# Projections of two small-head layers placed in steps without products with values, and tiles of ones written by ScalarE

## The reference

```python
# layer 1: 16 heads of 16, 256 queries, 256 keys, a mask on keys; then an MLP (gelu, 256 -> 1024 -> 256)
q = (LN(x) @ q_w + q_b); k, v = ctx @ k_w + k_b, ctx @ v_w + v_b
x = x + softmax(mask(q k^T / 4)) v @ cproj_w + cproj_b
x = x + gelu(LN(x) @ fc_w + fc_b) @ proj_w + proj_b
# layer 2: 16 heads of 16, queries from x, keys and values from concat(ctx, x): 512 keys
q = x @ q_w + q_b; k, v = concat(ctx, x) @ kv_w + kv_b
# layer 3: 32 query heads of 8 on 8 key heads, an additive mask, and a last LayerNorm
```

## Time and profile before

| | us |
|---|---|
| median of 3 runs | 1333.85 (1328.48 to 1335.38) |
| the profiled execution, its own time | 1333.88 |
| its span, first to last instruction | 1332.6 |
| TensorE busy in the span | 1280.4 (96%) |
| VectorE, ScalarE, GpSimd busy | 926.2, 744.4, 604.1 |
| mean granted TensorE clock | 0.981 |

### The profile page before, as it was taken

How to read it: one execution, slowest core, us unless ns; L and a number is a source line. 1 busy time by engine, 2 the same in 40 slices (tenths; PEclk the granted TensorE clock), 3 DMA queues, 4 the chain that set the end, 5 groups by cost and what they waited for, 6 DMA issues and landing times. The chain is left out here.

```text
span 1332.6 us, 27184 instructions
## 1 busy us (share of the span) xinstructions
PE 1280.4 (96%) x10005; PEld 1062.2 (80%) x10005; DVE 926.2 (70%) x2357; ACT 744.4 (56%) x1815; POOL 604.1 (45%) x969
## 2 busy tenths in 40 slices
PE   8999999999999999999899997999999898999997
PEld 7999999999999999999785555955655586666664
DVE  5887878788877777788667766566677365655663
ACT  5876666678766666668325563246555532544453
POOL 3874545468754545568515334133323221223323
PEclk9999999999999999999999999999998998999999
DMA  5530101124401010114112201220420202111000
GB/s 172 157 118 25 33 25 33 29 74 136 134 25 32 25 33 25 33 42 131 33 49 76 74 3 48 73 81 3 77 74 2 70 27 72 30 38 51 22 3 18
DMA packets 53364, 73.48 MB, mean 55 GB/s; under 512 B 11056, under 2 KB 25456, under 8 KB 53232
## 3 DMA queue, kind: packets, MB, share of 16 engines
q1 hardware_dynamic: 48112, 71.18, 18.1%
q0 software_dynamic: 5120, 0.56, 0.3%
HBM read 49.46 MB, written 1.05 MB: 38 GB/s over the span
## 5 line engine op out<-in xcount | busy, mean ns | idle before, releaser
L1063 POOL TENSOR_SCALAR E<-E,rl 128x256 f32<-128x256 f32 x256 | 243.2, 960 | 209.5 <-DVE rl L950 209.5
L2015 ACT ACTIVATE PT<-bank 128x512 f32<-128x512 f32 x320 | 184.5, 597 | 172.7 <-PE bank L1910 86.4
L2128 POOL DMA_DIRECT2D Q<-rows x160 | 90.1, 564 | 230.5 <-ACT rows L2029 226.0
L822 ACT ACTIVATE QTh<-bank,bqs 128x256 fp32r<-128x256 f32 x128 | 60.6, 474 | 155.3 <-PE bank L127 155.2
L2088 DVE CUSTOM_DVE_ANT_0 Em<-bank,M 128x256 bf16<-128x256 f32 x256 | 95.0, 420 | 74.7 <-issue 34.0
L1910 PE MATMUL bank<-Q,K 51*128 51x256 f32 (+1 forms) x640 | 130.3, 318 | 0.4 <-ACT PT L2015 0.3
L832 ACT ACTIVATE E<-bank,nm 128x257 f32<-128x257 f32 x256 | 119.3, 480 | 1.2 <-DVE nm L920 1.2
L2082 DVE TENSOR_REDUCE nm<-bank 128x1 f32<-128x512 f32 x128 | 86.6, 689 | 39.4 <-PE bank L1893 38.1
L954 DVE TENSOR_TENSOR PTl<-bank,PTh 128x512 fp32r<-128x512 f32 x128 | 87.9, 687 | 27.6 <-ACT PTh L844 27.1
L927 DVE SCALAR_TENSOR_TENSOR QTl<-bank,bqs,QTh 128x256 fp32r<-128x256 f32 x128 | 61.6, 481 | 62.8 <-ACT KT L823 62.0
L1957 PE MATMUL bank<-PT,V 128*32 128x256 f32 x1280 | 98.7, 402 | 2.1 <-ACT PT L2015 2.1
(11 more groups left out here) (434 smaller groups left out, 4526.2 us busy)
## 6 DMA issues: line engine op xcount, KB each, us to landing
stage<-in_wts SPq DMA_DIRECT2D x99, 256.0 KB, 3.3
U<-in_vrows SPq DMA_DIRECT2D x64, 256.0 KB, 2.7
Q<-stage SPq DMA_DIRECT2D x72, 128.0 KB
K<-stage SPq DMA_DIRECT2D x48, 128.0 KB
K<-xh SPq DMA_DIRECT2D x16, 128.0 KB, 3.1
Q<-rows POOLq DMA_DIRECT2D x96, 4.0 KB, 1.7
K<-stage SPq DMA_DIRECT2D x24, 64.0 KB
X<-in_x SPq DMA_DIRECT2D x4, 256.0 KB, 3.7
```

The source lines that it names most:

```text
L1063: m = pool.tensor_scalar(s.E[:, i % 3, t, 0:256], s.E[:, i % 3, t, 0:256], s.rl[:, r, t:t + 1], None, ALU.mult)
L2015: act.activation(s.PT[i % s.NPT][:, 2 * u:2 * u + 2, :].rearrange("p a b -> p (a b)"), s.STB[y][:], ACT.Exp).then_inc(S["t_ex"])
L2128: pool.dma_start(f32(s.Q[b % s.NR][at:at + 2, pair:pair + n, :]), f32(s.rows[4 * n * y:4 * n * y + 4 * n, g % 2, :])).then_inc(S[f"dma_row ...
```

## The change

1. `IN_LAYER` and `POSTS` give new steps to the projections of layers 1 and 2: q, k, x, v and c are in steps without products with values only. In layer 1 the values of batch b are now made in the first two steps of batch b itself, and the turn of the next batch's tokens is in the last step of the batch before.
2. The x projections of layer 2 (from the second batch on) go through bank `MB` in place of `PB`.
3. `keep_busy` issues nothing in steps that hold a projection or a post (one matmul in place of two in the first L steps), nothing in one more step of each group of products with values, and nothing in the drain.
4. The ones of the first batch's K, Q and V of each layer are copied by ScalarE in the MLP before, in parts of up to 1024 columns, in place of memsets by GpSimd. Those for Q and V of later batches are in parts of 1024 columns too.
5. A small exponential on a 2-column tile is issued by ScalarE two steps before the first real one.
6. Semaphore `ones_qv` is now `ones_q` and `ones_v`; the addition of the output bias (GpSimd) has a step name of its own, `res`; the memset of the mask row in layer 2 covers 256 columns in place of 512; GpSimd's memset of the third K tile of layer 1 is at step 8 in place of 6; the second batch's norm for MLP 1 is in steps 64 to 70 in place of 56 to 62.

```diff
-IN_LAYER = {1: {0: ["mask", "turn", "scale"], 1: ["th"], 2: ["tl", "k0"], 3: ["k1", "kh", "maskrow"],
-                4: ["kl", "k_out"], 5: ["q0", "mask_out"], 6: ["q1", "qh"], 7: ["ql", "q_out"], 9: ["v0"],
-                10: ["v1", "va"], 12: ["stats+"], 14: ["norm+"]},
-            2: {0: ["mask", "turn", "th"], 1: ["tl", "maskrow"], 3: ["q0"], 4: ["q1", "qh"], 5: ["ql"], 7: ["k0"],
-                8: ["k1", "kh"], 9: ["kl"], 11: ["x0"], 12: ["x1", "xh"], 13: ["xl"],
-                16: ["mask_out", "q_out", "k_out", "x_out"], 22: ["v0"], 23: ["v1", "va"], 26: ["v2"],
-                27: ["v3", "vb"]},
+IN_LAYER = {1: {0: ["mask", "v0-"], 1: ["v1-", "va-", "th", "res"], 2: ["tl"], 4: ["k0"], 5: ["k1", "kh"],
+                6: ["kl", "k_out"], 8: ["q0", "stats+"], 9: ["q1", "qh", "maskrow"], 10: ["ql", "q_out"],
+                12: ["mask_out", "norm+"], 15: ["turn+", "scale+"]},
+            2: {0: ["mask", "turn", "th"], 1: ["tl"], 2: ["res"], 4: ["q0"], 5: ["q1", "qh"], 6: ["ql", "maskrow"],
+                12: ["k0"], 13: ["k1", "kh"], 14: ["kl", "x0"], 15: ["x1", "xh"],
+                16: ["xl", "mask_out", "q_out", "k_out"], 17: ["x_out"], 20: ["v0"], 21: ["v1", "va"], 28: ["v2"],
+                29: ["v3", "vb"]},
...
-POSTS = {1: [["po0", "on0"], ["po1", "on1"], ["onT", "oth"], ["otl"], ["c0"], ["c1", "y"]],
-         2: [["po0", "on0"], [], ["po1", "on1"], [], ["onT", "oth"], ["otl"], [], ["c0"], ["c1", "y"]],
+POSTS = {1: {2: ["po0", "on0"], 3: ["po1", "on1"], 6: ["onT", "oth"], 7: ["otl"], 12: ["c0"], 13: ["c1", "y"]},
+         2: {2: ["po0", "on0"], 3: ["po1", "on1"], 5: ["onT", "oth"], 6: ["otl"], 18: ["c0"], 19: ["c1", "y"]},
...
+ONES_MLP = {1: {1: ("k", 0, 0), 2: ("k", 0, 1), 3: ("v", 0, 0), 4: ("q", 0, 0), 5: ("q", 0, 1)},
+            2: {0: ("k", 0, 0), 2: ("k", 0, 1), 3: ("k", 0, 2), 4: ("k", 0, 3), 5: ("v", 0, 0), 6: ("v", 0, 1),
+                8: ("q", 0, 0), 9: ("q", 0, 1)},
+            3: {2: ("k", 0, 0), 3: ("k", 0, 1), 4: ("v", 0, 0)}}
...
+def write_ones(c, s, table, n):
+    if n not in table[s.l]:
+        return
...
+    z = c.act.copy(dst[:, 1024 * part:min(columns, 1024 * part + 1024)].rearrange("p (a b) -> p a b", b=256),
+                   c.units[:].unsqueeze(1).broadcast_to([128, min(columns, 1024) // 256, 256]))
...
-def ones_first(c, s):
-    ones_keys(c, s, 0)
-    if s.l != 3:
-        c.pool.memset(f32(s.Q[0][:]), 1.0)
-    c.pool.memset(s.V[0][:], 1.0).then_inc(c.S["ones_qv"])
...
     def keep_busy(n):
         off, parts = MEET[l]
         g, k = divmod(n - s.L - off + 1, s.four)
-        start, end = n < s.L, n >= s.T
-        if n < 2 or n >= s.T + s.L or g > 0 and 0 < k <= parts or l == 3 and not start:
+        start = n < s.L
+        if n < 2 or n >= s.T or g >= 0 and k <= parts or l == 3 and not start:
             return
+        other = s.posts_at(n)[1] or any(x in ON_PE for b, x in s.preps(n) + s.norms(n))
+        if other and not start:
+            return
         w.wait_ge(S["m_x"], 4 * l)
-        w.wait_ge(S["t_os"], s.o["os"] + max(0, g if k else g - 1))
-        for _ in range(2 if start or end else 1):
+        w.wait_ge(S["t_os"], s.o["os"] + max(0, g))
+        for _ in range(2 if start and not other else 1):
...
+        if n == s.L - 2:
+            w.wait_ge(S["neghalf"], 1)
+            act.activation(c.tiny[:], c.neghalf, ACT.Exp)
```

More of the change, by code:

```diff
@@ L423, in mlp_sp @@
     for i in range(17):
-        for x in nxt.during(i):
-            heads_prep_sp(c, nxt, 0, x)
+        for b, x in nxt.during(i):
+            heads_prep_sp(c, nxt, b, x)
 def mlp_pe(c, s, prev, nxt):
@@ L516, in mlp_act @@
                 mlp_high(c, s, b)
-        for x in nxt.during(i):
-            heads_prep_act(c, nxt, 0, x)
+        for b, x in nxt.during(i):
+            heads_prep_act(c, nxt, b, x)
+        write_ones(c, nxt, ONES_MLP, i)
 def mlp_dve(c, s, prev, nxt):
@@ L1235, in take_rest, with x_bank, chosen @@
             self.Yo = sb("Yo", [128, 2, 2, 256])
+    def x_bank(self, b):
+        return self.MB if b else self.PB
     def all(self, n):
         return TILE_COUNTS[n][self.l - 1]
+    def chosen(self, b, steps):
+        steps = [(b + (x[-1] == "+") - (x[-1] == "-"), x.rstrip("+-")) for x in steps]
+        return [(b, x) for b, x in steps if b < NB]
     def during(self, i):
-        return IN_MLP[self.l].get(i, ())
+        return self.chosen(0, IN_MLP[self.l].get(i, ()))
     def preps(self, n):
-        b = n // self.TB + 1
-        return (b, IN_LAYER[self.l].get(n % self.TB, ())) if 0 < b < NB else (0, ())
+        if not 0 <= n < self.T:
+            return []
+        at = self.chosen(n // self.TB + 1, IN_LAYER[self.l].get(n % self.TB, ()))
+        if self.l == 1 and n == 0:
+            at = at + [(1, "turn"), (1, "scale")]
+        return [(b, x) for b, x in at if b > 0]
     def norms(self, n):
-        return NEXT_NORMS[self.l].get(n - 3 * self.TB, ()) if self.l < 3 else ()
+        return NEXT_NORMS[self.l].get(n - 3 * self.TB, []) if self.l < 3 else []
     def posts_at(self, n):
@@ L1348, in prep_bank_free @@
     order = HELD[l][min(b, 1)]
-    if x != order[0]:
+    if l == 1 and b:
+        if x == "t":
+            before, k = "q", k - 1
+        elif x == "q":
+            before = "k"
+        elif x == "v" and b + 1 < NB:
+            before, b = "t", b + 1
+        elif x == "v":
+            before = "q"
+        elif b == 1:
+            before = "t"
+        else:
+            before, k = "v", k - 1
+    elif x != order[0]:
         before = order[order.index(x) - 1]
@@ L1425, in heads_prep_sp @@
     elif x == "x_out":
[L1426 removed]
+        slot_free("k")
         K = s.K[r][:, :, 256:512]
@@ L1506, in heads_prep_act, with high @@
     hTh = c.hTh[:, :, 0:256]
-    def high(name, idx, bias, P, rows, n):
+    def high(name, idx, bias, P, rows, n, ps=s.PB):
         w.wait_ge(S["p" + name], idx + 1)
@@ L1630, in heads_prep_pool @@
         ln_rsqrt(pool, w, S, "ln", 12 + b, c.scr, 1e-5, c.neghalf)
-    elif x == "th":
+    elif x == "res":
         if l == 1:
@@ L1856, in heads_sp @@
     for n in range(s.steps()):
-        b, steps = s.preps(n)
-        for x in steps:
+        for b, x in s.preps(n):
             heads_prep_sp(c, s, b, x)
@@ L2095, in heads_dve @@
             maxima(k)
-        b, steps = s.preps(n - 1)
-        for x in steps:
+        for b, x in s.preps(n - 1):
             heads_prep_dve(c, s, b, x)
@@ L2137, in heads_pool @@
             maxima_parts(g)
-        if n == 6 and s.NR > 2:
+        if n == 8 and s.NR > 2:
             ones_keys(c, s, 2)
-        b, steps = s.preps(n - 2)
-        for x in steps:
+        for b, x in s.preps(n - 2):
             heads_prep_pool(c, s, b, x)
```

105 lines of the change are left out of this document (49 added, 56 removed), and 4 rows, old and new, of tables (IN_LAYER, POSTS).

## The result

| | before | changed |
|---|---|---|
| median | 1332.62 us (20 executions, 1327.98 to 1338.70) | 1333.94 us (20 executions, 1309.92 to 1346.82) |
| the profiled execution, time and span | 1333.88, 1332.6 | 1327.13, 1325.8 |
| its mean granted clock | 0.981 | 0.962 |
| granted clock, median over the executions | 0.982 | 0.958 |

Forecast were 1303 us and a range from 1292 to 1318. By them the change brought nothing. The new thing is the spread, 37 us instead of 11.

A forecast was written before the change was run, and what follows sets the result against it. TensorE's own instruction list was taken to pace layers 1 and 2. Layer 1 9.7, layer 2 16.9, MLPs 6.0, 0.4 and -0.5, clock -2.0 sum to 30.5 us off 1333.9: 1303 us, range 1292 to 1318.

The forecast's parts named there:

- the one on the clock: TensorE's clock: new short stops and lost fillers cost 2.0 us, one or two more slow stretches.
- 2.7 gained in MLP 1: MLP 1: with TensorE's hole gone, the half-clock stretch behind it probably goes too, 2.7 us.
- The rival of the clock: Layers 1 and 2: unused matmuls hold TensorE's clock; without them 110 us at half clock, 1347 us; chance 0.05.
- the threshold of 77 us for a loss: Layers 1 and 2: 77 us at half clock, at 0.42 lost each, would use up the gain.
- Fewer unused matmuls: Layers 1 to 3: 169 unused matmuls become 65, 0.32 us each where alone in a step; 27.8 us gained.
- Steps moved: Layers 1 and 2: projections in new steps shorten waits but add one for a DMA; -1.2 us in all.
- The wait at `ready`: Layer 1, step 16: TensorE waits for later query and mask DMAs, 2.4, 1.3 and 0.8 us by batch.
- Ones by ScalarE: MLPs: copies replace memsets and shorten TensorE's holes; without the clock 3.3, 0.4 and -0.5 us for MLPs 1, 0, 2.
- The layers: Lengths after the change: layer 1 95.6 us; layer 2 some 159 us instead of 175.7.
- another pacemaker: Layers 1 and 2: VectorE or the arrival of Q decides most steps, half the gain lost, 1317 us; chance 0.18.
- unused matmuls that turn into waits: The unused matmuls' time becomes equally long waiting for maxima, 1330 us; chance 0.05.
- mean clock in layers 1 and 2 below 0.95: Sign that would prove the forecast wrong: granted clock in layers 1 and 2 below 0.95.

The follow-up runs named there:

- e1: Changed kernel with the old rule for unused matmuls back (62 and 101 in layers 1 and 2): median 1329.47 us, ratio 0.9972.
- e2: Kernel before with only the new rule for unused matmuls (22 and 54 in layers 1 and 2): median 1326.31 us, ratio 0.9931.
- e7: Changed kernel with an earlier schedule for layer 1's first batch, without the stop ahead of step 16: median 1337.80 us, ratio 0.9956.
- e12: Changed kernel with all unused matmuls back and the earlier first batch of e7: median 1324.05 us, ratio 0.9935.
- e4: Kernel before with only the ones copied by ScalarE in the MLPs: median 1326.61 us, ratio 0.9957.
- e10: Changed kernel with the old rule for unused matmuls only up to the first product with values in layers 1 and 2: median 1323.72 us, ratio 0.9907.
- e13: e10 with the earlier first batch of e7, which takes away the stop: median 1329.52 us, ratio 0.9869.
- e17: e13 unaltered, run again for more executions: median 1327.59 us, ratio 0.9914.
- e14: e13 with the old rule for unused matmuls also from step 52 of layer 1 to its end: median 1315.58 us, ratio 0.9868.

## Why the prediction was wrong

**The step that failed** is the one on the clock: "I take 2.0 off for one or two more slow stretches of the shortest kind". Beside it stood 2.7 gained in MLP 1, so a clock as before was forecast. Measured is 0.024 less, 26 us by the slope. What the runs show in its place: with the 104 units back and all else kept the clock is 0.980 (e1), without them 0.958, so the units had been holding it; taken out of the old schedule they cost only 0.009 (e2), so the moved steps have a part in it. Two reasons stood behind the small number. "The fillers' places are taken by projections" does not hold where the clock falls: the fall of the changed kernel and of e7 at 717.50 lies in step 15 of layer 1, and steps 11 to 15 have no projection and steps 14 and 15 no unit (the last one ahead of the fall starts at 714.53 and 714.77). That "a stretch of products with values alone, with no filler, has the clock at 1.00" rested on a window of 3.10 us in a drain that had units all around it. It shows that such work can *run* at full clock behind units; it can't show that the clock lasts without them. Nor does layer 1 at 1.00 in the earlier trace rows speak against a fall: it was measured with the units.

**The rival of the clock** named the cause and was priced too rarely (0.05) and too high (1347, for 110 us at half clock in two layers). The mean clock says some 65 us more at half level than before (0.024 is 0.048 of 1333 us at half), and these cost 0.40 each, close to the 0.42 that came from steps at either level; the threshold of 77 us for a loss was of the right size, since 65 bring a zero. (The 270 us that it gives the two layers are 254 by its own sums, 95.6 and 158.8.) That the fall begins "behind each stop at `ready`" fits e1, where units stand; the changed kernel falls without that too (e7). The Trainium skill (TensorE: Matmul & The Clock Gate, "Why this matters for your kernels") warns of gaps between bursts of matmuls. The gaps that it names are longer than e1's stop of 1.90 us, and than the 2.4 us that the prediction gave its longest stop, so e1 and e12 agree with it in direction only; e7 goes beyond it, with no gap above 0.53 us ahead of its fall, and there the measurement decides.

**The terms of time were near.** Without the clock's items the forecast was 29.8 us, measured at equal clock 26.1.
- *Fewer unused matmuls*: 27.8 forecast, 21.1 measured (e1). A unit is worth 0.20 us in the mean, not 0.27: 0.32 was its price in a step without other work, but beside a projection or a post, where about half of those taken away stood (53 of 104), it is 1.58 less 1.33, 0.25. In steps 16 to 19 of layer 2 TensorE now waits for maxima, 0.61 and 0.74 us. I have not split the rest.
- *Steps moved*, with the wait that they bring: -1.2 forecast, +1.0 measured (e1 against e4). The wait at `ready` was 2.0, 0.7 and 0.5 us against 2.4, 1.3 and 0.8; working it out from the queue's rows was sound. Removing the first one brings 0.1 us at equal clock in e7 and 0.9 in e12, so it cost less than it lasted; what takes its place I did not trace.
- *Ones by ScalarE*: 3.2 forecast without the clock (3.3, 0.4 and -0.5), 4.0 measured (e4). Holes of 0.37 us in MLP 1 and 1.19 in MLP 0 were forecast at 0.7 and 1.33.
- *The layers.* Layer 1 was forecast at 95.6 us; measured are 110.9, and 38 us at half clock with 0.42 lost in each make 15.9 of that: 95.0. Layer 2: 159 forecast, 163.1 measured, 158.8 without its 10.2 us at half clock.

**The other rivals.** Neither another pacemaker nor unused matmuls that turn into waits: 21.1 us at equal clock are really gone. The point "mean clock in layers 1 and 2 below 0.95" was named as what would prove me wrong, and it did: 48 of 274 us at half clock are 0.91.

## What to carry to other kernels

Work that nobody needs can still hold TensorE's clock: before it goes, ask of each stretch what the clock there rests on, and take it away place by place. Compare two numbers, the time at equal clock and the clock, over a dozen executions, since one program's clock can differ by 0.03 between two of them; by the same token one trace shows where the clock can fall, not where it always does. Put unused matmuls at the places where the clock was seen to fall and leave them out elsewhere: 97 units in the two layers (1315.6 us) beat 163 (1324.1) and 61 (1334.8, both runs of the changed kernel). Whether taking a stop away helps too is not settled: it seems to from e1 to e12, and does not from e10 to e13 and e17.

## What the hardware showed that I had not expected

- The clock falls at short products with no wait above 0.53 us, and stays at half for up to 55 us of unbroken work; the changed kernel's executions ran from 0.945 to 0.979 with the same program.
- The busy time ahead does not sort the cases by itself: in the 4.00 us to 717.50, TensorE was busy 3.44 us in e7, which fell, and 3.49 in e14, which did not.
- Units half as wide cost 5.8 us at equal clock and came with a clock of 0.948, no higher than that of the kernel with hardly any (0.958).
- The start of layer 3 was at half clock for 24 us in the changed kernel and in e14, and for 14 in the kernel before (1120.2 to 1133.9); none of the edits was aimed at it, and why stays open.
